# Splitting the side products of an attention kernel in two, and reordering its first unit's DMA queue

## The chip, the core and the metric

The kernel runs on one core of a Trainium2 chip. The time is that of the device, in microseconds (us), as the median of several runs. TensorE (PE) multiplies matrices into PSUM, ScalarE (ACT) takes the exponentials, VectorE (DVE) and GpSimd (POOL) do the elementwise work, and SyncE (SP) issues nearly all DMAs, in program order.

## What is computed

x has 4 batches of 1024 rows of 128 numbers. The reference, cut to what matters:

```python
q, k, v = ln(x) @ Wq, ln(x) @ Wk, ln(x) @ Wv
latent  = (k + v) @ W_down_kv
k, v    = latent @ W_up_k, latent @ W_up_v           # 16 heads of 8
s       = clip(q @ k.T * scale) * exp(-c * |i - j|)   # per head, 1024 x 1024
x       = x + (softmax(s) @ v) @ Wo
x       = x + bf16(fp8(ln(x)) @ fp8(kernel)) + bias   # fp8 rounding, scales are 1
```

64 score matrices of 1024 x 1024 need 67 million exponentials; they are the bulk of the work.

## The kernel before

**Units and quads.** The work is cut into 8 units: unit 2b + h holds the 512 queries of half h of batch b. A unit has 4 groups of 4 heads, and a group has 8 key chunks of 128. One group with one chunk is a **quad**, so a unit has 32 quads, numbered 0 to 31 within it, and the program has 256. A quad has two **slots**, each with the scores of two heads: 128 keys x 1024. One ACT instruction (L758) exponentiates a slot. Three pairs of PSUM banks hold the slots in turn, so the scores of slot s can be made when the exponential of slot s - 3 has ended.

**A quad on PE** (the loop from L964 on) is: scores of the even slot (`qk`, two matmuls that run together), the product of probabilities and values of two quads ago (`weigh`, four matmuls in two passes, L957), scores of the odd slot, and then, where the table `PE_SIDE` has the quad, a **side product** (`job`). Side products are the projections of the next batch (T = transposes of the normalised rows, k, q, v, and n = sums of squares of all heads) and the tail of the unit before (sp = spread of the softmax sums over a head's columns, proj = product with Wo, xqT and y for the fp8 product). All of them use one PSUM bank, `work`, so each waits until DVE has emptied it of the one before (`emptied`); DVE does this one quad later (`DVE_SIDE`). v and proj are four fp32 matmuls of 128 columns, k, q and sp one fp32 matmul of 512 columns, n four of 32 output rows each side by side in the array, T four transposes.

**The decay** is folded into queries and keys. It is exact off the diagonal block. In quads whose keys lie in the queries' own half (the even quads of a unit), DVE multiplies part of the scores by a correction before the exponential may start (`fix`, L1182): 2 x 256 columns in quads 2 and 4 of a group, here called **wide**, and 2 x 128 in quads 0 and 6, **narrow**. Odd quads need none.

**Group ends.** When the eight quads of a group are weighed, DVE copies the sums out of PSUM (`copy_pv`, L1190), and the first `weigh` of the next group, which stands in its quad 2, that is in quads 2, 10, 18 and 26 of a unit, waits for this copy. SP then sends the copy to tiles `den` and `o_raw` in 8 small DMAs (`gather`, L453 and L456). In quad 7 of the next unit DVE waits for the last of them, inverts the sums (L1195) and widens them (L1201); the corrections of quad 8 stand behind that on DVE.

**SP's queue** is written out by hand. In unit 0 it holds the gathers of each group, the stores of the keys and queries of batch 0 and 1 in three bf16 parts (L390, L398), and the loads that stage them for the groups (`stage`, L405, L413). **POOL** makes these parts (`split`), the normalised rows, and the end of the fp8 product. Before L698 it does, per batch: early keys and queries, the result of the unit before, late keys, late queries, squares for n.

## Time and profile before

| | |
|---|---|
| median of 3 runs | 534.98 us (530.42 to 535.65) |
| the profiled execution's own time | 534.09 us |
| its span, first to last instruction | 532.2 us |
| PE busy | 490.4 us (92%) |
| ACT busy | 490.8 us (92%), 512 exponentials |
| DVE, POOL busy | 280.6 and 218.8 us |
| mean granted TensorE clock | 0.985 |

PE and ACT are both busy 92% of the span. That is an average. A busy PE is read with care, since a matmul's record runs on while the next has begun; what counts for PE is the distance between the starts of successive blocks.

### The profile page before, as it was taken

To read this page: it belongs to the slowest core of one execution; us is meant where nothing else is said; L and a number is where in the kernel's file an instruction comes from. 1 tells how busy PE (TensorE), PEld (TensorE's weight loads), DVE (VectorE), ACT (ScalarE), POOL (GpSimd) and SP (SyncE) were. 2 spreads that over 40 slices of the span, in tenths; PEclk is the share of its full clock that TensorE was granted. 3 is DMA by queue.
4 is the path that set the end of the run, shared out by engine and by line. 5 is a ranking of instruction groups with operands and counts; after the bars stand their busy time and mean duration, and the time that the engine had idled before them with its cause. 6 is when DMAs were issued, how large, how long until landed. Compare 5 with 4: busy or idle time off the path is not lost.

```text
span 532.2 us, 9397 instructions
## 1 busy us (share of the span) xinstructions
PE 490.4 (92%) x3457; PEld 113.2 (21%) x3457; DVE 280.6 (53%) x641; ACT 490.8 (92%) x534; POOL 218.8 (41%) x285
## 2 busy tenths in 40 slices
PE   7799999899999999999999999999999999999961
PEld 3312111131122212221121211221111212122220
DVE  4524744455645564554744555554555645455646
ACT  3789999889999999999999999999999999999961
POOL 0889419791450229992251218993101211002110
PEclk9999999899999999999999999999999999999995
DMA  5589789837976102757967000757977000100000
GB/s 174 166 253 223 254 240 261 315 144 175 249 158 149 46 5 71 263 183 192 263 149 178 10 4 23 278 169 214 264 176 166 20 7 7 46 1 2 1 20 25
DMA packets 50467, 73.79 MB, mean 139 GB/s; under 512 B 6192, under 2 KB 29168, under 8 KB 50416
## 3 DMA queue, kind: packets, MB, share of 16 engines
q1 hardware_dynamic: 49600, 72.85, 49.5%
q8 instruction: 29, 0.48, 0.4%
q10 hardware_dynamic: 816, 0.28, 0.2%
q14 instruction: 22, 0.18, 0.1%
HBM read 35.40 MB, written 35.65 MB: 133 GB/s over the span
## 4 chain that ended last, share of the span: by engine, by line
PE 45%; ACT 34%; issue 9%; DVE 5%; DMA 3%; POOL 2%; SPq 1%; ACTq 0%; DVEq 0%; POOLq 0%
ACT probs L758 33%; PE ps L957 23%; PE ps L941 13%; DVE ps L1182 2%; PE ps L937 2%; PE ps L859 1%; PE ps L854 1%; PE ps L822 1%; PE ps L831 1%; DMA decay<-decay_rows 1%; PE ps L826 1%; DMA o_raw<-pv_out 1%; DMA wuv_s<-L_attn_W_up_v 1%; SPq L453 0%; POOL sq L584 0%
## 5 line engine op out<-in xcount | busy, mean ns | idle before, releaser
L758 ACT ACTIVATE probs<-ps 128x1024 f32<-128x1024 f32 x512 | 480.2, 1067 | 14.9 <-DVE ps L1182 9.4
L957 PE MATMUL ps<-probs,V 128*9 128x512 f32 x2048 | 268.6, 596 | 3.0 <-ACT probs L758 0.8
L1182 DVE TENSOR_TENSOR ps<-ps,consts 128x256 f32<-128x256 f32 (+1 forms) x256 | 143.9, 565 | 176.3 <-PE ps L941 169.3
L941 PE MATMUL ps<-Qs,Ks 64*128 64x512 bf16 x992 | 181.7, 386 | 16.6 <-ACT probs L758 8.4
L941 PEld LDWEIGHTS ps<-Qs,Ks 64*128 64x128 bf16 x992 | 43.9, 93 | 288.8 <-ACT probs L758 272.1
L645 POOL TENSOR_TENSOR xs<-xs,magic 128x512 f32<-128x512 f32 x7 | 8.9, 1277 | 96.2 <-DVE magic L1243 96.2
L957 PEld LDWEIGHTS ps<-probs,V 128*9 128x9 f32 x2048 | 31.3, 88 | 77.9 <-issue 57.6
L1190 DVE COPY pv_out<-ps 105x512 f32<-105x512 f32 x31 | 21.4, 691 | 33.7 <-PE ps L957 33.7
L562 POOL TENSOR_SCALAR rs<-mv 128x4 f32<-128x4 f32 (+1 forms) x10 | 2.3, 229 | 82.7 <-DVEq L1364 82.0
L596 POOL TENSOR_TENSOR sq<-sq,parts 128x1024 f32<-128x1024 f32 (+1 forms) x16 | 29.0, 1813 | 1.3
L598 POOL TENSOR_TENSOR parts<-sq,parts 128x1024 bf16<-128x1024 f32 (+1 forms) x16 | 28.3, 1771 | 1.3
L658 POOL TENSOR_TENSOR yb<-yb,bias_s 128x512 bf16<-128x512 bf16 x7 | 8.1, 1154 | 49.6 <-DVE yb L1315 49.2
L584 POOL TENSOR_TENSOR sq<-kT,decay 128x512 f32<-128x512 f32 (+2 forms) x13 | 16.2, 1246 | 28.5 <-DVE kT L1282 26.6
L589 POOL TENSOR_TENSOR sq<-qT,decay 128x1024 f32<-128x1024 f32 x7 | 16.6, 2366 | 3.5 <-DMA qp_dram<-parts 2.3
L595 POOL CAST parts<-sq 128x1024 bf16<-128x1024 f32 (+1 forms) x16 | 14.9, 933 | 1.0
L597 POOL CAST parts<-sq 128x1024 bf16<-128x1024 f32 (+1 forms) x16 | 14.4, 897 | 1.0
L937 PE MATMUL ps<-Qs 32*128 32x512 f32 x64 | 9.1, 637 | 3.2 <-ACT probs L758 2.6
L826 PE MATMUL ps<-xnT,wq_s 128*128 128x512 f32 x16 | 9.0, 643 | 0.8 <-ACT xnT L737 0.8
L822 PE MATMUL ps<-xnT,wk_eff 128*128 128x512 f32 x16 | 8.9, 638 | 0.8 <-ACT qT L743 0.8
L831 PE MATMUL ps<-wv_eff,xnT 128*128 128x128 f32 x64 | 9.3, 288 | 0.0
L646 POOL TENSOR_TENSOR xs<-xs,magic 128x512 f32<-128x512 f32 x7 | 8.9, 1278 | 0.5
L1098 DVE BATCH_NORM_STATS2 stats<-X 128x6 f32<-128x128 f32 x32 | 6.8, 278 | 3.3 <-DMA X<-L_attn_x 3.2
(148 smaller groups left out, 284.7 us busy)
## 6 DMA issues: line engine op xcount, KB each, us to landing
Qs<-qp_dram SPq DMA_DIRECT2D x26, 512.0 KB, 9.2
qp_dram<-parts SPq DMA_DIRECT2D x14, 768.0 KB, 4.6
Ks<-kp_dram SPq DMA_DIRECT2D x26, 384.0 KB, 5.5
kp_dram<-parts SPq DMA_DIRECT2D x12, 384.0 KB, 3.5
kp_dram<-parts SPq DMA_DIRECT2D x6, 768.0 KB, 5.2
qp_dram<-parts SPq DMA_DIRECT2D x7, 512.0 KB, 6.0
X<-L_attn_x SPq DMA_DIRECT2D x10, 256.0 KB, 3.3
Qs<-qp_dram SPq DMA_DIRECT2D x10, 256.0 KB, 9.5
```

The lines of the kernel that those rows point to most:

```text
L584: chain(nc.gpsimd.tensor_tensor(rest[:, at:at + n], kT[:, cols], decay[:, 1 - v, cols], ALU.mult))
L589: chain(nc.gpsimd.tensor_tensor(rest.rearrange("p (v n) -> p v n", v=2), q2, decay[:, :, cols], ALU.mult))
L595: chain(nc.gpsimd.tensor_copy(to[0], r))
L596: chain(nc.gpsimd.tensor_tensor(r, r, to[0], ALU.subtract))
L598: chain(nc.gpsimd.tensor_tensor(to[2], r, to[1], ALU.subtract))
L758: nc.scalar.activation(probs[:, quad % RING, 2 * jp:2 * jp + 2, :].rearrange("p j n -> p (j n)"), ps_all[:, bank * CH:(bank + 2) * CH], AC ...
L831: last = nc.tensor.matmul(bank[:, t * P:(t + 1) * P], xnT[:, at:at + P], wv_eff[:, :], start=True, stop=True)
L937: last = nc.tensor.matmul(bank, K0[group, g, kc * P:(kc + 1) * P], Q0[group, v, :], start=True, stop=True)
L941: last = nc.tensor.matmul(bank, Ks[half, g, jp, key_cols(v, kc)], Qs[half, g, jp, qh, v, :], start=True, stop=True)
L957: last = nc.tensor.matmul(pv[32 * j:32 * j + VW, :], V[:, unit // 2 * NB + kc, HG * j + g, :], probs[:, quad % RING, j, :], start=i == 0, ...
L1182: nc.vector.tensor_tensor(own, own, factors, ALU.mult).then_inc(fixed, 1)
L1190: nc.vector.tensor_copy(pv_out[0:96 + VW, group % 2, :], pv[0:96 + VW, :]).then_inc(pv_copied, 1)
```

## The change

Four things are changed.

1. **Split side products.** k, q, v, n, sp and proj (all but those of the first projections) are issued in two parts: the first and the second 256 columns, two of the four column blocks, or two of n's four matmuls. An entry of `JOBS` now has two places. A place that ends in .5 lies inside the quad that begins half a quad later, right behind the scores of its even slot and ahead of `weigh`. Only the last part signals, so DVE empties the bank once, as before.
2. **Other places.** Parts within a quad stand in quads 2, 10, 18 and 26. In a unit of the middle with odd number the places are: q at 2 (inside) and 2 (end), xqT at 4, y at 6, sp at 10 (inside, end), proj at 12 and 14, v at 18 (inside, end), the second v at 20 and 22, n at 26 (inside, end). With even number: xqT at 2 (inside), y at 4, T at 6, sp at 10 (inside, end), proj at 12 and 14, T at 18 (inside), k at 20 and 22, the second k at 26 (inside, end), q at 28 and 30. Row statistics of the tail move from 13 and 15 to 15 and 17, the last unit's transposes (`turn`) from 14, 18 and 26 to 18 (inside), 22 and 26 (inside), and the flags from 14 and 18 to 18 and 20.
3. **SP's queue in unit 0.** Late queries of batch 0 are stored before the gather of group 1 and not behind it; the early keys of batch 1 behind the gather of group 3 and not ahead of it; x of batch 2 is loaded behind the gather of group 2 and not ahead of that of group 1.
4. **POOL and DVE.** POOL makes the late keys before the result of the unit before, for batches 2 and 3. The preparation of the fp8 weights on DVE moves from quads 16 to 23 of unit 0 to 21 to 28.

```diff
-JOBS = [(FIRST_VALUES, "v", 0), (3, "v", 1), (10, "q", 1), (22, "n", 0)]
+JOBS = [(None, FIRST_VALUES, "v", 0), (None, 3, "v", 1), (None, 10, "q", 1), (20, 22, "n", 0)]
...
-        (10, "sp"), (12, "proj"), (TAIL_ROWS[_u], "xqT"), (TAIL_PRODUCTS[_u], "y"))]
+        (9.5, 10, "sp"), (12, 14, "proj"), (None, _rows, "xqT"), (None, _products, "y"))]
...
@@ SP, unit 0
                     store_qk(0)
+                    store_queries(0, "late queries", 1)
                 elif g == 1:
-                    store_queries(0, "late queries", 1)
...
-                    if qh == 0 and g == 2 and b < B - 1:
+                    if qh == 0 and g == (3 if b == 0 else 2) and b < B - 1:
                         store_keys(b + 1, "early keys", early, 0)
...
-                    if qh == 0 and g == 0 and b < B - 2:
+                    if qh == 0 and g == (2 if b == 0 else 0) and b < B - 2:
                         sp.wait_ge(tr_ps, 2 * b + 2)
                         load_x(b + 2)
@@ POOL
                     early_parts(b + 1)
+                    late_keys(b + 1)
                     if b > 0:
                         result(2 * b - 1)
-                    late_keys(b + 1)
@@ PE
+            def project_k(n, bank, part=None):
+                if part != 1:
+                    pe.wait_ge(xnT_ready, n + 1)
+                last = nc.tensor.matmul(columns(bank, part), wk_eff[:, :], xnT[:, own_rows(n, part)], start=True, stop=True)
+                if part != 0:
+                    last.then_inc(k_ps, 1)
...
+                for a in range(2) if part is None else (part,):
                     for half in range(2):
                         at = 64 * a + 32 * half
                         last = nc.tensor.matmul(bank[at:at + 32, :], hsum, sq[:, a, half * CH:(half + 1) * CH],
                                                 start=True, stop=True)
...
                     qk(s)
+                    if s % 2 == 0 and quad - 0.5 in PE_SIDE:
+                        job(*PE_SIDE[quad - 0.5])
                     if quad >= 2 and s % 2 == in_f32:
                         weigh(quad - 2)
...
@@ DVE
-                elif at == 13:
+                elif at == 15:
                     row_stats(unit)
-                elif at == 15:
+                elif at == 17:
...
-                if 16 <= quad < 24:
-                    prepare_weights(quad - 16)
+                if 21 <= quad < 29:
+                    prepare_weights(quad - 21)
```

What this does to the order of the instructions is shown at three places. The first is PE in unit 3, from quad 9 on. `ps<-Qs,Ks` are scores (x2 is one slot), `ps<-probs,V` is `weigh`, `ps<-wide,consts` is sp and `ps<-wo_s,OT` is proj. Before:

```order
L941 MATMUL ps<-Qs,Ks 128x512 x4
L957 MATMUL ps<-probs,V 9x512 x4
L941 MATMUL ps<-Qs,Ks 128x512 x2
L854 MATMUL ps<-wide,consts 128x512
L941 MATMUL ps<-Qs,Ks 128x512 x2
L957 MATMUL ps<-probs,V 9x512 x4
L941 MATMUL ps<-Qs,Ks 128x512 x4
L957 MATMUL ps<-probs,V 9x512 x4
L941 MATMUL ps<-Qs,Ks 128x512 x2
L859 MATMUL ps<-wo_s,OT 128x128 x4
L941 MATMUL ps<-Qs,Ks 128x512 x2
```

Changed:

```order
L972 MATMUL ps<-Qs,Ks 128x512 x4
L880 MATMUL ps<-wide,consts 128x256
L988 MATMUL ps<-probs,V 9x512 x4
L972 MATMUL ps<-Qs,Ks 128x512 x2
L880 MATMUL ps<-wide,consts 128x256
L972 MATMUL ps<-Qs,Ks 128x512 x2
L988 MATMUL ps<-probs,V 9x512 x4
L972 MATMUL ps<-Qs,Ks 128x512 x4
L988 MATMUL ps<-probs,V 9x512 x4
L972 MATMUL ps<-Qs,Ks 128x512 x2
L888 MATMUL ps<-wo_s,OT 128x128 x2
L972 MATMUL ps<-Qs,Ks 128x512 x2
```

Half of sp now stands ahead of quad 10's `weigh`, half behind its second scores, and half of proj where all of it stood. The second place is PE in unit 3 where n stands (`ps<-sq,consts`), before in quad 28:

```order
L957 MATMUL ps<-probs,V 9x512 x4
L941 MATMUL ps<-Qs,Ks 128x512 x2
L840 MATMUL ps<-sq,consts 32x512 x4
L941 MATMUL ps<-Qs,Ks 128x512 x2
L957 MATMUL ps<-probs,V 9x512 x4
```

Changed, in quad 26:

```order
L972 MATMUL ps<-Qs,Ks 128x512 x4
L863 MATMUL ps<-sq,consts 32x512 x2
L988 MATMUL ps<-probs,V 9x512 x4
L972 MATMUL ps<-Qs,Ks 128x512 x2
L863 MATMUL ps<-sq,consts 32x512 x2
L972 MATMUL ps<-Qs,Ks 128x512 x2
L988 MATMUL ps<-probs,V 9x512 x4
```

The four matmuls that stood together stand two and two, on both sides of a `weigh`. The third place is SP's queue in unit 0, behind the stores of k and q of batch 0. Before:

```order
L433 DMA kt_dram<-kT 128x1024
L435 DMA qt_dram<-qT 128x1024
L363 DMA X<-L_attn_x 128x8x128
L453 DMA den<-pv_out 8x1x64
L456 DMA o_raw<-pv_out 8x512
```

Changed:

```order
L436 DMA kt_dram<-kT 128x1024
L438 DMA qt_dram<-qT 128x1024
L401 DMA qp_dram<-parts 128x3x1024 x2
L401 DMA qp_dram<-parts 128x2x1024
L456 DMA den<-pv_out 8x1x64
L459 DMA o_raw<-pv_out 8x512
```

The store of the late queries has come ahead of the gather of group 1, and the load of x has gone from there.

## Rows read from the trace of the kernel before

**Rows 1.** Windows, units 1, 3, 4: length, busy PE, PEld, DVE, ACT, POOL, clock, DMA.

```profile
84.04:148.56 64.52, 60.35 (x426) 13.28 (x422) 34.00 (x78) 60.23 (x66) 39.48 (x50) 0.97 0.81 227
209.18:270.12 60.94, 58.94 (x426) 13.34 (x424) 33.97 (x79) 60.09 (x65) 38.93 (x51) 1.00 0.77 225
270.12:330.75 60.63, 59.20 (x422) 13.18 (x420) 32.48 (x65) 60.04 (x65) 20.27 (x28) 1.00 0.27 62
```

**Rows 2.** Timeline, ACT without gap: start, length, engine, line, operation, tiles, count.

```profile
373.23 14.85 ACT L758 ACTIVATE probs<-ps 128x1024 f32<-128x1024 f32 x16
```

**Rows 3.** Timeline of a wide quad (20 of unit 5), no side product near.

```profile
369.27 0.92 PE L941 MATMUL ps<-Qs,Ks 64*128 64x512 bf16 x4
369.70 0.70 DVE L1182 TENSOR_TENSOR ps<-ps,consts 128x512 f32<-128x512 f32 x1 [0.60 <-PE ps L941]
370.52 1.06 ACT L758 ACTIVATE probs<-ps 128x1024 f32<-128x1024 f32 x1
```

**Rows 4.** Groups by form: line, engine, shapes, count, busy us, mean ns, idle before.

```profile
L1182 DVE TENSOR_TENSOR ps<-ps,consts 128x256 f32<-128x256 f32 x128 | 54.8, 432 | 98.5 <-PE ps L941 95.9 <-PE ps L937 2.1 <-DVE mv L1224 0.5
```

**Rows 5.** Timeline of PE, unit 5: sp in quad 10, proj in quad 12.

```profile
349.94 1.12 PE L854 MATMUL ps<-wide,consts 128*128 128x512 f32 x2
350.47 0.59 PE L854 MATMUL ps<-wide,consts 128*128 128x512 f32 x1
351.00 0.39 PE L941 MATMUL ps<-Qs,Ks 64*128 64x512 bf16 x2
352.30 0.61 PE L941 MATMUL ps<-Qs,Ks 64*128 64x512 bf16 x4
353.81 0.39 PE L941 MATMUL ps<-Qs,Ks 64*128 64x512 bf16 x2
354.13 1.16 PE L859 MATMUL ps<-wo_s,OT 128*128 128x128 f32 x8
355.22 0.39 PE L941 MATMUL ps<-Qs,Ks 64*128 64x512 bf16 x2
```

**Rows 6.** Timeline of PE: n in unit 5; T in unit 4.

```profile
384.25 1.06 PE L840 MATMUL ps<-sq,consts 128*32 128x512 f32 x8
385.25 0.39 PE L941 MATMUL ps<-Qs,Ks 64*128 64x512 bf16 x2
304.15 0.65 PE L816 MATMUL ps<-eye,X 128*128 128x128 f32 x4
```

**Rows 7.** Timeline of quad 18 of unit 5: the copy at a group's end.

```profile
363.91 0.69 DVE L1190 COPY pv_out<-ps 105x512 f32<-105x512 f32 x1 [0.78 <-PE ps L957]
364.23 0.10 PEld L941 LDWEIGHTS ps<-Qs,Ks 64*128 64x128 bf16 x2 [0.37 <-ACT probs L758]
364.75 0.62 PE L957 MATMUL ps<-probs,V 128*9 128x512 f32 x4
```

**Rows 8.** Timeline of the stall in quad 8 of unit 1.

```profile
99.20 0.55 DVE L1195 RECIPROCAL rec<-den 128x64 f32<-128x64 f32 x1 [1.63 <-DMA o_raw<-pv_out]
99.61 1.16 POOL L596 TENSOR_TENSOR sq<-sq,parts 128x512 f32<-128x512 f32 x1
99.79 1.53 DVE L1201 TENSOR_TENSOR wide<-rec,consts 128x512 f32<-128x512 f32 x1
101.76 1.02 ACT L758 ACTIVATE probs<-ps 128x1024 f32<-128x1024 f32 x1 [2.23 <-DVE ps L1182]
```

**Rows 9.** Timeline of SP's queue; last row from the chain of waits.

```profile
63.85 2.07 SPq L398 DMA_DIRECT2D qp_dram<-parts  x3
70.92 1.32 SPq L405 DMA_DIRECT2D Ks<-kp_dram  x2
...
87.44 2.00 SPq L390 DMA_DIRECT2D kp_dram<-parts  x3
...
94.27 4.84 DMA o_raw<-pv_out
```

**Rows 10.** Timeline of unit 0: one DVE step of `prepare_weights`.

```profile
54.53 1.60 DVE L1150 TENSOR_SCALAR xs<-w_s,rscales 128x128 f32<-128x128 bf16 x1
```

More of the change, by code:

```diff
@@ L3 @@
 from contextlib import ExitStack
+import math
 F32 = mybir.dt.float32
@@ new lines @@
+    JOBS += [(_b * STREAM + 57.5, _b * STREAM + 58, "n", _b + 1)]
+JOBS += [(None, 3 * STREAM + 18, "flags", 0), (None, 3 * STREAM + 20, "flag", 0)]
+JOBS += [(None, (UNITS - 1) * UNIT_QUADS + _q, "turn", _g) for _g, _q in enumerate((17.5, 22, 25.5))]
+JOBS.sort(key=lambda _j: _j[1])
+LOOPED_UNITS = 2 * B
+JOB_ORDER = [(_k, _i) for _, _, _k, _i in JOBS] + [(_k, UNITS + _n) for _n in range(LOOPED_UNITS) for _k in ("proj", "xqT", "y")]
+PE_SIDE = {_q: (_k, _i, None if _f is None else 1) for _f, _q, _k, _i in JOBS}
@@ L146, in build @@
+PE_SIDE.update({_f: (_k, _i, 0) for _f, _, _k, _i in JOBS if _f is not None})
+assert len(PE_SIDE) == len(JOBS) + len([_j for _j in JOBS if _j[0] is not None])
+DVE_SIDE = {math.ceil(_q) + (_q > FIRST_VALUES): (_k, _i) for _, _q, _k, _i in JOBS}
+assert len(DVE_SIDE) == len(JOBS)
 def build(nc, x, wq, wkT, wvT, wo, wd, wuk, wuv, w8, s_in, s_k, bias, decay_rows, decay_table,
@@ L832, in project_v, with head_norms @@
                                             start=True, stop=True)
-                last.then_inc(v_ps, 1)
-            def head_norms(b, bank):
-                pe.wait_ge(sq_ready, b + 1)
-                for a in range(2):
+                if part != 0:
+                    last.then_inc(v_ps, 1)
+            def head_norms(b, bank, part=None):
+                if part != 1:
+                    pe.wait_ge(sq_ready, b + 1)
+                for a in range(2) if part is None else (part,):
                     for half in range(2):
@@ L841, in head_norms @@
                                                 start=True, stop=True)
-                last.then_inc(n_ps, 1)
+                if part != 0:
+                    last.then_inc(n_ps, 1)
             def turn_tops(bank):
@@ L850, in sum_oks, with spread_sums, project_o @@
                 nc.tensor.matmul(bank[0:1, 0:1], oks[:, 0:1], ones[:, :], start=True, stop=True).then_inc(flag_ps, 1)
-            def spread_sums(unit, bank):
-                pe.wait_ge(spread, unit + 1)
-                nc.tensor.matmul(bank, same_head, wide[:, :], start=True, stop=True).then_inc(spread_ps, 1)
-            def project_o(unit, bank):
-                pe.wait_ge(ot_ready, unit + 1)
-                for t in range(4):
+            def spread_sums(unit, bank, part=None):
+                if part != 1:
+                    pe.wait_ge(spread, unit + 1)
+                cols = slice(0, CH) if part is None else half_cols[part]
+                last = nc.tensor.matmul(bank[:, cols], same_head, wide[:, cols], start=True, stop=True)
+                if part != 0:
+                    last.then_inc(spread_ps, 1)
+            def project_o(unit, bank, part=None):
+                if part != 1:
+                    pe.wait_ge(ot_ready, unit + 1)
+                for t in range(4) if part is None else pairs[part]:
                     last = nc.tensor.matmul(bank[:, t * P:(t + 1) * P], OT[:, unit % 2, t * P:(t + 1) * P], wo_s[:, :],
                                             start=True, stop=True)
-                last.then_inc(proj_ps, 1)
+                if part != 0:
+                    last.then_inc(proj_ps, 1)
             def transpose_xq(unit):
@@ L902, in job @@
                 elif kind == "sp":
-                    spread_sums(i, work)
+                    spread_sums(i, work, part)
                 elif kind == "turn":
@@ L907, in job @@
                 elif kind == "proj":
-                    project_o(i, work)
+                    project_o(i, work, part)
                 elif kind == "xqT":
@@ L998, in _ @@
             weigh(QUADS - 1)
-            pairs = (range(0, 2), range(2, 4))
             for half in range(2):
```

56 lines of the change are left out of this document (25 added, 31 removed).

## The prediction

> **What bounds the kernel now.** I read the page first: ACT and PE are each busy 92% of the span, so neither can be called the bound from the averages. The windows by unit come next [rows 1]: units 3 and 4, in the steady part, last 60.94 and 60.63 us, unit 1 64.52. Against these stands ACT without a gap: 16 exponentials in 14.85 us, of which the last alone is about 1.06 us, so one each 0.92 us and 64 in 58.7 us [rows 2]. A middle unit loses 2.0 to 2.3 us to waits, unit 1 5.9 us. Only these losses can be won, and ACT's pace is the floor.
>
> Where they arise needs the timeline of a quad without side work [rows 3]. Two exponentials are 1.83 us, which is ACT's pace for a quad. On PE, in a quad where PE is late the step from scores to scores takes 352.30 to 353.81, 1.51 us [rows 5]. So PE catches up **0.31 us per quad**, and every side product makes it late. How late may it be? In the wide quad the correction of the odd slot ends at 369.70 + 0.70 = 370.40 and the exponential starts at 370.52; I take 0.03 of these 0.12 for the signal. The odd slot of a **wide** quad thus forgives **0.09 us**. A **narrow** correction lasts 0.43 and not 0.70 [rows 4], so it forgives 0.27 more; I use 0.31. An **uncorrected** quad forgives 0.70 more than the wide one, 0.80.
>
> **An account by hand.** Let D be PE's lateness at a quad's start. A side product at the end of a quad adds its own time plus 0.09 (scores to scores take 0.23, scores to side product 0.32 [rows 5]) and takes off 0.31 of recovery. What D exceeds the allowance of the next quads by is paid by ACT and leaves D. Before, sp takes 351.00 - 349.94 = 1.06, proj 355.22 - 354.13 = 1.09 [rows 5], n 1.00 [rows 6]. For sp in 10 and proj in 12: quad 10 pays 0.1 for the copy at the group's end and is 0.16 later by it; quad 11 D = 0.90, pays 0.10; wide quad 12 D = 0.49, pays 0.40; quad 13 pays 0.16; narrow 14 0.18. Sum 0.94. A second v in 14 pays 0.38 + 0.18, q and v in 4 and 6 of odd units 0.04 + 0.18 + 0.38 + 0.18, n in 28 only 0.16, because its next corrected quad is narrow. The whole account gives 2.6 for an odd unit and 2.35 for an even one; the trace has 2.3 and 2.0 [rows 1]. It is high by 0.3 in both, so I use differences alone.
>
> **The split parts.** A 512-column fp32 product is two passes, which start at 349.94 and 350.47, and the next scores follow at 351.00 [rows 5]. Each pass is 0.53. I estimate 0.43 of it for the 512 columns (two cycles each at the granted 2.4 GHz) and 0.10 as fixed, a weight load or the change to the next block. Half of its columns cost 0.10 + 0.43 + 0.10 = 0.63, so two parts are 1.26: splitting adds 0.2 us of PE time to each. Half a proj or v is 0.64. Bounds: 0.53 (exactly half) and 0.75 (every overhead doubled); I take 0.63 because the load stands in front of each of these products. n is different: its four matmuls run side by side in 1.00 us [rows 6], so two of them should take 1.00 as well, bounds 0.5 and 1.0; n doubles, to 2.0 us.
>
> **Parts inside quads 2, 10, 18, 26.** There PE waits for the copy: scores at 364.24, copy ends 363.91 + 0.69 = 364.60, `weigh` starts 364.75, which is 0.51 behind the scores and not 0.32 [rows 7]. The hole is only 0.19 us wide. A part of 0.63 in it delays `weigh` by 0.63 against a quad without either, and with it the odd scores of a *wide* quad, which forgives 0.09. ACT pays 0.54 at once, 0.91 for half an n, about 0.5 for T (its record is 0.65 [rows 6], some 0.06 of it beside the next block) and 0.24 for xqT (0.33). Afterwards PE is less late, which is what the spacing wins.
>
> - **sp and proj now**: quad 10 pays 0.54; the end part leaves D = 0.50 in quad 11, 0.19 in 12, which pays 0.10; proj's halves in 12 and 14 never pass the allowance (0.51 in 13, 0.63 in 15, 0.32 in 16, pays 0.01). Sum 0.65, was 0.94.
> - **Odd unit**: q in 2 with xqT, y behind it 0.64; sp, proj 0.65; v in 18, 20, 22 0.68; n 0.91 in quad 26, 0.08 in 27, 0.40 in wide 28, 1.39 in all, was 0.16. Sum 3.35, was 2.6: **+0.75** each for units 3 and 5.
> - **Even unit**: xqT 0.24, T in 6 nothing, sp, proj 0.65, T in 18 0.50, k in 20, 22 nothing, k in 26 0.54, q in 28, 30 0.10. Sum 2.03, was 2.35: **-0.3** each for units 2 and 4.
> - **Unit 6**: xqT 0.24 is new, 0.3 is won at sp and proj, and the flags' chain of small DVE steps now delays a wide quad (20) where it delayed a narrow one (16): **+0.2**. **Unit 7**: the transposes inside 18 and 26, of T's size, pay about 0.5 each, the latter after a copy it waits for; 0.3 won at sp: **+0.6**.
> - **Unit 0**: the weights' steps leave quads 16 to 23, where one of them took 1.60 us for 128 columns [rows 10] with corrections queued behind it; I put that at 0.8 us. At 21 to 28 POOL is idle. The k and q products of quads 26 to 30 cost 0.64 for 1.4; T inside 18 costs 0.5, n in halves 0.6 for 0.1. **-0.6**.
> - Row statistics two quads later leave POOL four quads (7.3 us) for 14 small steps of 0.3 us: nothing. POOL's late keys ahead of the result: late queries start at about the same time, since y is two to four quads later; nothing.
>
> **The stall in unit 1.** DVE stood 1.63 us until the last gather of unit 0 landed at 99.11 (94.27 + 4.84 [rows 9]); then came 0.55, and 1.53 for the widening, over twice its usual time. The exponential of quad 8 started 2.3 us late [rows 8]. PE idled, and in this unit the granted clock is 0.97 of full [rows 1], that is 3.4 us at 1.2 GHz, the lower of its two levels; it cost about 1.2 us in quads 10 and 11. Together 3.5 us, the estimate that unit 1's length against unit 3's confirms (64.52 - 60.94 = 3.6). In the new order the store of the late queries stands one gather (5.4 us of issue) and one load ahead of 63.85, so the staging loads, which wait for it, start some 3 us before 70.92. The last gather then does not wait for the 2.0 us issue of the early keys at 87.44 either, nor lie behind their 2 MB [rows 9]. I estimate its issue complete by 92 and its landing at 95 to 97, and DVE wants it at about 97.6. The wait goes.
>
> What is late next is the widening. It started at 99.79 while a POOL step ran until 99.61 + 1.16 = 100.77, and ended 0.55 behind that step [rows 8]: DVE stood until POOL was through. In the new order k's last projection of batch 1 comes two quads later, so POOL is then splitting the early queries in steps of up to 2.1 us. DVE has 0.3 us to spare; a mean wait of about 1 us plus 0.55 leaves a stall of about 1.3 us, too short for the clock to fall. Bounds 0 and 2.2. Unit 1 also gets the odd unit's +0.8. So 1.3 + 0.8 - 3.5: **-1.4**.
>
> By the Trainium skill, page "SBUF — State Buffer", section "Who interferes with whom", a DVE instruction with two SBUF inputs and a GpSimd one exclude each other for their whole length. The trace agrees (100.77 and then 0.55), and it is this rule that speaks for a rest of the stall.
>
> **Sum**: -0.6 - 1.4 - 0.3 + 0.75 - 0.3 + 0.75 + 0.2 + 0.6 = -0.3. Against the profiled execution's 534.1 us this is **533.8 us**. The median shown is 0.9 above that execution; I keep its own time.
>
> By the Trainium skill, "TensorE: Matmul & The Clock Gate", section "LDWEIGHTS" and its mechanism in Part 3, PE pulls weight loads ahead of running matmuls where row groups allow. Here the trace disagrees: the second pass starts 0.53 behind the first for 0.43 of columns [rows 5]. The rule would make the loads vanish behind the columns; what that gives is the rival of parts of exactly half.
>
> **Rivals.**
> - **As summed** (532 to 535.5), 0.40.
> - **The parts inside hide** (0.17). If the hole under load is longer than 0.19, since DVE's copy is later when PE is, a part of 0.63 pays 0.2 and not 0.54. There are 27 such parts in the 8 units; 27 x 0.25 = 6.8 us less: 527. Against it: rows 6 are quads where PE was on time, as it mostly is there.
> - **Parts of exactly half** (0.05): a part's fixed 0.10 is hidden, it costs 0.53 and not 0.63, 0.1 less at each of the 27 inside parts: 2.7 us less, 531. Against it stand both passes of 0.53.
> - **The stall goes wholly** (0.18): POOL's step ends in time. 1.3 us less, 532.5.
> - **Slower: the stall stays whole** (0.15). Its place is quad 8 of unit 1, its price the 2.1 us that I counted as won, and it decides once widening ends over 2.3 us late, by a late landing or a long POOL step. Then only the steady loss is left: 536. With the parts at 0.75 as well (0.12 more at some 27 places) 539.5.
> - **The change doesn't spread anything** (0.05): a second part waits for the bank's emptying. It doesn't by the code, which waits for first parts alone; time as before.
>
> **Chances.** What can be told from no change is about 1%, 5.3 us. Faster than 529.6 takes the hidden parts (0.17), or parts of half with the stall wholly gone and the bounds on its side (0.04): 0.21. Slower than 540.3 needs the whole stall and dear parts: 0.05. Within: 0.74. The range for 8 in 10 runs from 528.5, inside the hidden case, to 537.5.
>
> **What would show it.** After: exponentials of the odd slot in quads 2, 10, 18, 26 start 0.5 us late; blocks of n of 1.0 us each, twice; sp's halves 0.63 apart; units 3 and 5 longer by 0.7, unit 1 shorter by 1.4; no clock loss near 104; DVE's widening in unit 1 over 1 us. The prediction is wrong if `weigh` behind an inside part starts within 0.7 us of the scores, or if n's halves take 0.5.

## The result, and the profile after

The changed kernel takes 536.28 us (median, 533.6 to 539.36) and the kernel before 533.37 us (530.42 to 536.65) on the same chip: ratio 1.0044, 95% interval 1.0027 to 1.0061. By the medians that is 2.9 us slower, by the ratio 2.3 us (it is not the quotient of the two medians, which is 1.0055), where I forecast 0.3 us less. The time lies inside my range (528.5 to 537.5), but the sign is wrong, and a ratio of 1 lies outside the interval. The profiled execution of after is the longest of its 20: 539.36 us, span 537.5 us, 5.3 us above the 534.1 of the profiled execution before. I keep the two scales apart: terms are compared between traces, the whole between medians. So the stall that this trace shows below may be larger than what the median execution loses.

The page after, the instructions and the exponentials in section 5:

```profile
PE 496.2 (92%) x3495; PEld 119.6 (22%) x3495; DVE 275.9 (51%) x641; ACT 487.3 (91%) x534; POOL 219.1 (41%) x285
...
L763 ACT ACTIVATE probs<-ps 128x1024 f32<-128x1024 f32 x512 | 476.6, 1068 | 24.1 <-DVE ps L1212 20.6
```

ACT stands idle ahead of the exponentials for 24.1 us, where it was 14.9. 20.6 of it is put down to corrections (L1212), before it was 9.4. Which corrections these are, the windows by unit tell; they are to be compared with [rows 1]. Units 1 to 4, columns as there:

```profile
83.22:145.33 62.11, 60.48 (x434) 14.48 (x430) 34.14 (x79) 59.63 (x66) 43.83 (x54) 1.00 0.73 211
145.33:212.56 67.23, 61.93 (x424) 14.50 (x422) 31.89 (x64) 59.63 (x66) 19.43 (x27) 0.95 0.38 86
212.56:274.65 62.09, 60.30 (x438) 14.52 (x434) 34.06 (x80) 59.62 (x65) 39.90 (x52) 1.00 0.76 223
274.65:335.20 60.55, 59.18 (x424) 14.04 (x422) 32.01 (x64) 59.30 (x66) 19.43 (x27) 1.00 0.27 61
```

Unit 1 is 2.4 us shorter than before, unit 3 1.15 us longer, unit 4 as before, and **unit 2 lasts 67.23 us where it lasted 60.63**, with the granted clock at 0.95. All eight, each from its first exponential (L763, before L758) to the next unit's, unit 7 to the end of the last:

```
unit         0      1      2      3      4      5      6      7
before   68.46  64.51  60.63  60.94  60.63  60.94  60.00  59.76
after    68.06  62.11  67.23  62.09  60.55  61.69  59.46  60.37
differs  -0.40  -2.40  +6.60  +1.15  -0.08  +0.75  -0.54  +0.61
forecast -0.6   -1.4   -0.3   +0.75  -0.3   +0.75  +0.2   +0.6
```

Unit 2 alone misses its term by 6.9 us. The other seven sum to -0.9, against a forecast of 0.0 for these seven.

The stall of unit 1 [rows 8] is gone. Timeline of its quad 7 and 8 after:

```profile
96.42 0.54 DVE L1225 RECIPROCAL rec<-den 128x64 f32<-128x64 f32 x1
96.56 1.04 POOL L602 CAST parts<-sq 128x1024 bf16<-128x1024 f32 x1
96.99 1.15 DVE L1231 TENSOR_TENSOR wide<-rec,consts 128x512 f32<-128x512 f32 x1
97.67 2.46 POOL L603 TENSOR_TENSOR parts<-sq,parts 128x1024 bf16<-128x1024 f32 x1
98.06 0.42 DVE L1212 TENSOR_TENSOR ps<-ps,consts 128x256 f32<-128x256 f32 x1
```

The reciprocal has no wait in brackets any more. The widening takes 1.15 us, not 0.69: a POOL step runs beside it until 97.60, and it ends 0.54 us behind that step. The correction of quad 8 stands behind it, and ACT still runs through fifteen exponentials without a gap (from 89.30 to 103.26). In its place stands a new stall, a unit later. Timeline of quad 8 of unit 2:

```profile
162.78 0.55 DVE L1225 RECIPROCAL rec<-den 128x64 f32<-128x64 f32 x1 [4.82 <-DMA o_raw<-pv_out]
163.37 0.69 DVE L1231 TENSOR_TENSOR wide<-rec,consts 128x512 f32<-128x512 f32 x1
163.98 0.76 DVE L1212 TENSOR_TENSOR ps<-ps,consts 128x256 f32<-128x256 f32 x2
164.50 4.69 ACT L763 ACTIVATE probs<-ps 128x1024 f32<-128x1024 f32 x5 [4.11 <-DVE ps L1212]
...
166.50 0.61 PE L972 MATMUL ps<-Qs,Ks 64*128 64x512 bf16 x2 [0.31 <-ACT probs L763]
167.03 1.22 PE L880 MATMUL ps<-wide,consts 128*128 128x256 f32 x2
...
168.19 1.90 PE L988 MATMUL ps<-probs,V 128*9 128x512 f32 x8
```

DVE stands for 4.82 us until the last gather of unit 1 has landed, ACT for 4.11. Then the clock goes: half of sp takes 1.22 us and not 0.70, a `weigh` of eight 1.90 and not 1.05. One window over it, 164 to 174 us; the third number from the end is the granted clock, and behind it stands the busy share of the DMA engines:

```profile
164.00:174.00 10.00, 8.11 (x36) 1.90 (x40) 3.62 (x8) 7.08 (x8) 0.00 (x0) 0.66 0.31 84
```

The granted clock is 0.5 of full, the 1.2 GHz level, for 6.8 us from 165.2 (0.34 of the 10 us is missing, at half clock 6.8 us), after PE had idled through the stall. Quad 8 lasts 6.04 us and not 1.83, which is the wait, 4.2 us; quads 10 to 12 last 4.15, 2.18 and 2.25 where they last 2.34, 1.83 and 1.93 at full clock (unit 4 after), which is the clock's part, 2.5 us.

Why the gather landed so late stands in SP's queue and in the chain of waits. Timeline of SP, then the end of the chain in front of the stall:

```profile
145.17 1.31 SPq L408 DMA_DIRECT2D Ks<-kp_dram  x2
146.53 1.25 SPq L416 DMA_DIRECT2D Qs<-qp_dram  x2
147.82 0.70 SPq L456 DMA_DIRECT2D den<-pv_out  x1
```

```profile
152.66 10.03 DMA o_raw<-pv_out
```

A gather of 16 KB that took 4.84 us to land before, in the stall of unit 1 [rows 9], took 10.03. The staging loads of batch 1's second half (L408, L416; 1.8 MB) are issued right ahead of it. In the kernel before, the same gather was issued at 155.73, 3.1 us later, and had landed when DVE came for it at 159.98. So the gather is not issued late; what has grown is its time from issue to landing. The DMA engines are busy all of this time, from 145 to 163 us (share 1.03, next to last):

```profile
145.00:163.00 18.00, 16.20 (x124) 3.71 (x120) 6.67 (x12) 15.29 (x17) 5.32 (x5) 1.00 1.03 223
```

### The profile page after: what moved, and what is told of

Read it like the earlier page. It is cut to its first block, busy times and chain, and to the rows that moved or that the text cites. A ratio compares the mean times of both kernels' runs of the same rounds, so it can differ in the third digit from the quotient of the medians.

```text
span 537.5 us, 9480 instructions
## 1 busy us (share of the span) xinstructions
PE 496.2 (92%) x3495; PEld 119.6 (22%) x3495; DVE 275.9 (51%) x641; ACT 487.3 (91%) x534; POOL 219.1 (41%) x285
## 4 chain that ended last, share of the span: by engine, by line
PE 44%; ACT 32%; issue 9%; DVE 6%; DMA 4%; POOL 3%; SPq 2%; DVEq 0%; POOLq 0%; ACTq 0%
ACT probs L763 31%; PE ps L988 22%; PE ps L972 13%; DMA o_raw<-pv_out 2%; PE ps L880 2%; DVE ps L1212 2%; PE ps L844 1%; PE ps L851 1%; PE ps L863 1%; PE ps L839 1%; PE ps L888 1%; DMA Ks<-kp_dram 1%; DMA kp_dram<-parts 1%; DMA X<-L_attn_x 1%; PE ps L821 1%
## 5 line engine op out<-in xcount | busy, mean ns | idle before, releaser
L763 ACT ACTIVATE probs<-ps 128x1024 f32<-128x1024 f32 x512 | 476.6, 1068 | 24.1 <-DVE ps L1212 20.6
L1212 DVE TENSOR_TENSOR ps<-ps,consts 128x256 f32<-128x256 f32 (+1 forms) x256 | 144.1, 566 | 194.1 <-PE ps L972 186.6
L972 PE MATMUL ps<-Qs,Ks 64*128 64x512 bf16 x992 | 179.0, 386 | 18.1 <-ACT probs L763 11.3
L650 POOL TENSOR_TENSOR xs<-xs,magic 128x512 f32<-128x512 f32 x7 | 8.9, 1277 | 69.1 <-DVE magic L1273 69.1
L600 POOL CAST parts<-sq 128x1024 bf16<-128x1024 f32 (+1 forms) x16 | 14.9, 932 | 1.0
L844 PE MATMUL ps<-xnT,wq_s 128*128 128x256 f32 (+1 forms) x28 | 10.6, 460 | 0.8 <-ACT xnT L742 0.8
L839 PE MATMUL ps<-xnT,wk_eff 128*128 128x256 f32 (+1 forms) x28 | 10.5, 458 | 0.8 <-ACT qT L748 0.8
L851 PE MATMUL ps<-wv_eff,xnT 128*128 128x128 f32 x64 | 10.9, 297 | 0.0
L880 PE MATMUL ps<-wide,consts 128*128 128x256 f32 x28 | 10.8, 472 | 0.0
L888 PE MATMUL ps<-wo_s,OT 128*128 128x128 f32 x56 | 10.0, 300 | 0.0
```

Source lines behind the costliest of these rows:

```text
L763: nc.scalar.activation(probs[:, quad % RING, 2 * jp:2 * jp + 2, :].rearrange("p j n -> p (j n)"), ps_all[:, bank * CH:(bank + 2) * CH], AC ...
L844: last = nc.tensor.matmul(columns(bank, part), wq_s[:, :], xnT[:, own_rows(n, part)], start=True, stop=True)
L851: last = nc.tensor.matmul(bank[:, t * P:(t + 1) * P], xnT[:, at:at + P], wv_eff[:, :], start=True, stop=True)
L880: last = nc.tensor.matmul(bank[:, cols], same_head, wide[:, cols], start=True, stop=True)
L972: last = nc.tensor.matmul(bank, Ks[half, g, jp, key_cols(v, kc)], Qs[half, g, jp, qh, v, :], start=True, stop=True)
L1212: nc.vector.tensor_tensor(own, own, factors, ALU.mult).then_inc(fixed, 1)
```

## The experiments

**What the theories were.** Theory 1, for unit 2: the stall needs three things at once. The compute is 3.2 us earlier (unit 2 starts at 145.33, before at 148.56); POOL makes batch 1's k and q parts later, because in the new table k's second product of unit 0 is in quad 30 and q's first in 34, where they were in 28 and 30; and the staging loads lie ahead of the gather. The rivals: the new queue order does it alone, or the split work does. Theory 2, for the +1.15 in odd units: n is doubled by the split. Theory 3: parts inside quads 2, 10, 18, 26 are a loss by themselves, and the same work spaced apart elsewhere would be free.

Each ratio is to the kernel before on the same chip, but the experiments ran on three chips: the first four on one, queue_late_stage, n_whole, t_end and spread_q on a second, sp_spaced and q_spaced on a third. The kernel before took 533.68, 534.08 and 534.24 us there. A difference of medians across two of these groups therefore carries some 0.5 us that is not the kernel's, and where I give one, the lengths of the units in the two traces say more.

### Split jobs with the old queue

The changed kernel, with SP's order as it was:

```diff
-                    store_queries(0, "late queries", 1)      # ahead of the gather of group 1
+                    store_queries(0, "late queries", 1)      # behind it
...
-                    if qh == 0 and g == (3 if b == 0 else 2) and b < B - 1:
+                    if qh == 0 and g == 2 and b < B - 1:
...
-                    if qh == 0 and g == (2 if b == 0 else 0) and b < B - 2:
+                    if qh == 0 and g == 0 and b < B - 2:
```

> The changed kernel with SP's queue of unit 0 as it was before. Theory 1 (the changed kernel loses 4.8 us in quad 8 of unit 2 because the last gather of unit 1 lands behind staging loads, after POOL's parts and with them the whole queue came 3.6 us later and compute 3.3 us earlier): unit 1 stalls again as before (64.5 to 66 us long), so that compute comes later and the stall in unit 2 shrinks to 0 to 2 us; median 535 to 538. Rival (the new order of SP's queue by itself makes the stall in unit 2): unit 2 is 60.5 us, with no wait for a gather, and the median is 534 to 535.5.

539.59 us (539.57 to 539.62), ratio 1.0118 [1.009, 1.0147]: the slowest of all, above the 535 to 538 expected. Unit 2 is back at 60.54 without a wait: it starts at 151.50, 6.2 us later than in the changed kernel. Unit 1 has the stall, larger than before the change (68.59 us). Timelines of DVE and of SP's queue, then the gather in the chain of waits:

```profile
100.97 0.55 DVE L1224 RECIPROCAL rec<-den 128x64 f32<-128x64 f32 x1 [4.78 <-DMA o_raw<-pv_out]
```

```profile
90.34 2.02 SPq L393 DMA_DIRECT2D kp_dram<-parts  x3
```

```profile
98.91 1.97 DMA o_raw<-pv_out
```

The stall's return to unit 1 was foretold, its size not. The store of the early keys, ahead of the last gather, starts at 90.34 where it was at 87.44 [rows 9]: 2.9 us later. The last gather behind it is issued 4.6 us later, lands 1.8 us later (100.9, before 99.1) and is wanted 1.4 us earlier (96.2, before 97.6), which gives 4.78 us of wait where it was 1.63. So the later products of k feed straight into unit 1, and the new queue order is what keeps them out of it.

### The queue alone

The kernel before with only the three changes on SP (the diff above, the other way).

> The kernel before with only SP's queue of unit 0 in the new order. Theory 1: the stall in unit 1 goes (unit 1 61.0 us, not 64.5), POOL is not late, so the last gather of unit 1 lands near 158 where compute wants it at 156.6; a stall in unit 2 of 0 to 1.5 us; median 1.5 to 3.5 us under the kernel before. Rival (the queue's order makes the stall): unit 2 loses 4 us or more in quad 8, median as before or over it.

531.28 us (530.21 to 533.78), 0.9964 [0.9945, 0.9983]. Unit 1 goes from 64.51 to 61.08. Unit 2 goes from 60.63 to 61.39: a small stall has come up there, and the granted clock stays full. ACT stands 0.78 us in it, DVE 2.34:

```profile
158.46 0.55 DVE L1195 RECIPROCAL rec<-den 128x64 f32<-128x64 f32 x1 [2.34 <-DMA o_raw<-pv_out]
```

Unit 2 starts at 144.60, 4.0 us earlier than before, and POOL is not later (the late queries are stored at 114.68, before at 114.39). So earlier compute alone brings the landing of unit 1's last gather into the path (wanted at 156.1, before at 159.98; it takes 6.59 us to land), and the queue order is worth about 2 us as it is. Unit 1's gain of 3.4 us is what its stall was worth; I had put it at 3.5.

### The gather ahead of the staging loads

The changed kernel; staging of group 2 of batch 1 waits until the last gather is issued:

```diff
-                    if qh == 1 and b < B - 1:
+                    if qh == 1 and b < B - 1 and not (b == 0 and g == 2):
                         sp.wait_ge(qk_done, 2 * NB * (group + 1))
+                        if b == 0 and g == 3:
+                            stage(b + 1, 2)
                         stage(b + 1, g)
```

> The changed kernel, with the staging loads of group 2 of batch 1 issued behind the last gather of unit 1 and not ahead of it. Theory 1: the gather has one group's loads (2 x 384 and 2 x 512 KB) less before it, lands near 154, ahead of need (158), and unit 2 falls from 67.2 to 60.5 us with the clock at its full level throughout; median 5 us under the changed kernel's slow executions and 3 to 4 us under its median. Rival (POOL or the copy is what is late, not the loads ahead): unit 2 keeps over 3 us of its stall.

532.54 us (531.96 to 533.02), 0.9988 [0.9972, 1.0004]. Unit 2 is 60.54, its clock full, and no other unit has moved by more than 0.2 us except unit 0, -0.3:

```profile
144.94:205.49 60.55, 59.19 (x424) 14.06 (x422) 32.00 (x64) 59.30 (x66) 19.47 (x27) 1.00 0.39 90
```

The loads ahead of the gather were needed for the stall: it is issued at 152.04, 0.6 us earlier than in the changed kernel, and no wait for it is left. The median falls by 3.7 us, and the times of single runs, spread over 5.8 us in the changed kernel, now lie within 1.1. That fits a landing that decides by a small margin in each run whether there is a stall; it is an argument, since only one execution of each is traced.

### k and q of unit 0 whole and earlier

The changed kernel, with the k and q products of batch 1 unsplit, and all but the first two to four quads earlier:

```diff
-        ... (20 if _b else 25.5, 22 if _b else 26, "k", 0),
-        (25.5 if _b else 28, 26 if _b else 30, "k", 1), (28 if _b else 33.5, 30 if _b else 34, "q", 0),
-        (33.5 if _b else 36, 34 if _b else 38, "q", 1), ...
+        ... (20 if _b else None, 22 if _b else 26, "k", 0),
+        (25.5 if _b else None, 26 if _b else 28, "k", 1), (28 if _b else None, 30, "q", 0),
+        (33.5 if _b else None, 34 if _b else 36, "q", 1), ...
```

> The changed kernel with batch 1's k and q products whole and where they were before (quads 26, 28, 30, 36), so that POOL can make the parts of batch 1 some 3 us earlier. Theory 1: SP's gather of group 0 of unit 1 starts near 116.5 and not 120, the last gather of unit 1 lands 3 to 4 us earlier, and the stall in unit 2 falls from 4.8 to 1.5 us or less; unit 0 with its three products close together loses 0.8 us more; median 1 to 3 us under the changed kernel. Rival (the order of the queue alone): the stall keeps over 3.5 us.

532.92 us (532.41 to 536.55), 0.9996 [0.9977, 1.0016]; unit 2 60.55, no wait. The median is 3.4 us under the changed kernel's, where I expected 1 to 3. One range end, 536.55, is not explained by the traced execution. The first POOL step on k's second product stands in these timelines, of before, of the changed kernel and of this one:

```profile
78.08 2.63 POOL L584 TENSOR_TENSOR sq<-kT,decay 128x256 f32<-128x256 f32 x2 [18.11 <-DVE kT L1282]
```

```profile
81.30 2.63 POOL L589 TENSOR_TENSOR sq<-kT,decay 128x256 f32<-128x256 f32 x2 [21.75 <-DVE kT L1312]
```

```profile
77.50 2.63 POOL L589 TENSOR_TENSOR sq<-kT,decay 128x256 f32<-128x256 f32 x2 [17.97 <-DVE kT L1312]
```

Two quads of PE (3.66 us) make POOL 3.2 us later, and that runs on through SP: the store of batch 1's late queries, in unit 1, is at 114.39 before, 118.04 in the changed kernel, 113.75 here, and what is behind it follows: three gathers and the staging loads. The loads next ahead of the last gather start at 145.17 in the changed kernel and at 141.24 here. The last gather itself is issued at nearly the same time in both, 152.66 and 152.43: here SP waits for DVE's copy before it, in the changed kernel it comes to it straight from the loads. What the earlier loads give it is DMA engines that have room. DVE of this version, and its window 150 to 158:

```profile
157.73 0.54 DVE L1225 RECIPROCAL rec<-den 128x64 f32<-128x64 f32 x1
```

```profile
150.00:158.00 8.00, 7.64 (x64) 1.90 (x56) 4.14 (x9) 7.94 (x9) 2.32 (x2) 1.00 0.73 166
```

DVE comes at 157.73 and does not wait, so the gather took at most 5.3 us where it took 10.03; by the trace's completion records it landed at 157.41, 0.3 us before it was wanted. This cure holds by a small margin, which would fit the one execution of 536.55, though that one was not traced.

Either cure suffices, so the stall of 4.8 us needs both POOL's lateness and the loads ahead of the gather. That it needs the earlier compute too is seen in split_old_queue, where unit 2 starts late and has no stall. Neither rival holds: the new queue order by itself gives a small stall, the split work with the old order none in unit 2. Theory 1 holds, with one correction: compute that is earlier still (4.0 us, queue_only) brings 2.34 us of DVE's wait, 0.78 of ACT's, without POOL's lateness.

### The queue alone, with the gather ahead

queue_only with the staging edit.

> The kernel before with SP's queue of unit 0 in the new order, and the staging loads of group 2 of batch 1 behind the last gather of unit 1; side products as before. Theory (both stalls are the last gather's landing, nothing else): no wait for a gather in units 1 and 2, unit 1 61.0 us, unit 2 60.6 us instead of 61.4, median 0.7 to 1 us under that with the new queue alone, so 3 to 3.5 us under the kernel before. Rival (loads behind the gather are then late for quad 16 of unit 2): a new wait on a DMA in unit 2, no gain.

530.63 us (530.13 to 530.98), 0.9941 [0.9919, 0.9964]. Unit 2 is 60.63 as before, unit 1 61.09. This is what the queue's part of the change is worth once its own follow-up stall is taken out: 3.45 us of median. It also weighs the split jobs with their new places: with the same queue, late_stage takes 532.54, 1.9 us more between two chips (1.6 by the sum of the eight units).

### n in one piece

From here every kernel has the staging edit. n goes back to quad 28 (unit 0: 22), unsplit:

```diff
-JOBS = [... (20, 22, "n", 0)]
+JOBS = [... (None, 22, "n", 0)]
...
-    JOBS += [(_b * STREAM + 57.5, _b * STREAM + 58, "n", _b + 1)]
+    JOBS += [(None, _b * STREAM + 60, "n", _b + 1)]
```

> The changed kernel with the staging loads behind the gather, and n whole again, at the end of quad 28 (22 in unit 0). Theory 2 (half an n takes as long as a whole one, and its first half delays a wide quad at once): units 1, 3 and 5 fall from 62.1 to 60.8 us, unit 0 by 0.4 us, median 3.5 to 4.5 us under the kernel with n in halves, near 528.5. Rival (halves cost half, the loss of odd units comes from the parts of q, sp and v inside quads): under 1 us.

528.84 us (527.76 to 529.07), 0.9900 [0.987, 0.9931]. Against late_stage units 1, 3 and 5 shorten by 1.3, 1.3 and 1.05, 3.6 us in all; the medians, on two chips, differ by 3.7. Unit 0 shortens by 0.1 where I expected 0.4. Unit 3:

```profile
204.29:265.10 60.81, 59.47 (x438) 14.37 (x434) 34.09 (x80) 59.51 (x66) 39.58 (x51) 1.00 0.76 223
```

PE's busy time in it is 0.8 us less than in the changed kernel (60.30). n in the changed kernel, unit 5, timeline of PE:

```profile
382.59 0.90 PE L972 MATMUL ps<-Qs,Ks 64*128 64x512 bf16 x4
383.42 0.62 PE L863 MATMUL ps<-sq,consts 128*32 128x512 f32 x2
383.58 0.60 PE L988 MATMUL ps<-probs,V 128*9 128x512 f32 x2
383.87 0.60 PE L863 MATMUL ps<-sq,consts 128*32 128x512 f32 x2
384.01 1.32 PE L988 MATMUL ps<-probs,V 128*9 128x512 f32 x6
385.26 0.39 PE L972 MATMUL ps<-Qs,Ks 64*128 64x512 bf16 x2
385.58 1.05 PE L863 MATMUL ps<-sq,consts 128*32 128x512 f32 x4
386.57 0.39 PE L972 MATMUL ps<-Qs,Ks 64*128 64x512 bf16 x2
```

The half at the end stands from 385.58 to 386.57: 0.99 us for two matmuls, as long as the 1.00 of all four [rows 6]. Theory 2 holds.

### T, xqT and the transposes at the ends of quads

On top of it:

```diff
-    _rows, _products = (28, 30) if not is_shared(_u) else (33.5, 36) if _u % 2 else (36, 38)
+    _rows, _products = (28, 30) if not is_shared(_u) else (34, 36) if _u % 2 else (36, 38)
...
-        ... (None, 17.5, "T", 1), ...
+        ... (None, 18, "T", 1), ...
...
-... for _g, _q in enumerate((17.5, 22, 25.5))]
+... for _g, _q in enumerate((18, 22, 26))]
```

> As the one with n whole, and everything that was whole but stood inside quads 2, 18 and 26 (xqT, T, the last unit's transposes) now at the end of the same quads. No splitting is changed. Theory 3 (an inside part delays the odd scores of a wide quad, which forgives 0.09 us, by its full length; the hole at the group's end covers 0.19): units 2 and 4 fall by 0.5 to 0.6 us, unit 6 by 0.2, unit 7 by 0.6, unit 0 by 0.3; median 2 to 2.5 us lower. Rival (the hole hides inside parts, so at the end they cost more): same or slower.

525.31 us (525.05 to 526.23), 0.9845 [0.9815, 0.9875]. Units 2 and 4 lose 0.6 us each (4: 60.48 to 59.88), unit 7 0.8, unit 0 1.1, unit 6 0.2: 3.5 us of median, more than expected. The window of unit 4 and, from the page, the exponentials:

```profile
263.35:323.23 59.88, 59.12 (x424) 13.96 (x422) 32.00 (x64) 59.09 (x65) 19.95 (x28) 1.00 0.30 68
```

```profile
L765 ACT ACTIVATE probs<-ps 128x1024 f32<-128x1024 f32 x512 | 474.8, 1071 | 11.7 <-DVE ps L1214 9.0
```

ACT's idle time ahead of them is 11.7 us, against 24.1 in the changed kernel and 14.9 before. Quad 18 with T at its end lasts 1.85 us, with T inside 2.29: the same operation costs 0.02 at the free end beside the place where it cost 0.46, and 0.06 in quad 20.

### q at two ends, and y out of the way

```diff
-    _rows, _products = (28, 30) if not is_shared(_u) else (34, 36) if _u % 2 else (36, 38)
+    _rows, _products = (28, 30) if not is_shared(_u) else (34, 36) if _u % 2 else (34, 40)
...
-        (33.5 if _b else 36, 34 if _b else 38, "q", 1), ...
+        (36, 38, "q", 1), ...
```

> As the one before, and in odd units the second q in halves at the ends of quads 4 and 6, xqT at the end of 2 and y at the end of 8, so nothing stands inside quad 2. The account by hand gives odd units 3 and 5 0.1 us for 0.64 there: 0.5 us less each, 1 us less in all, near 525.5. Rival (POOL's result, late by y's two quads, makes late queries late): no gain, waits on POOL's parts in SP's queue.

526.65 us (525.95 to 527.05), 0.9866 [0.9836, 0.9896]: 1.3 us more than t_end, where 525.5 was expected (units 3 and 5 are 0.4 us longer each). Quads 0 to 7 of units 3 and 5 are free of any loss (1.83 us each), as the theory said. But quad 10 went from 2.34 to 3.34. Its timeline:

```profile
219.40 0.69 DVE L1222 COPY pv_out<-ps 105x512 f32<-105x512 f32 x1 [1.22 <-PE ps L990]
220.00 0.74 DVE L1347 TENSOR_SCALAR yb<-ps,oscale 128x512 bf16<-128x512 f32 x1
220.66 0.69 DVE L1214 TENSOR_TENSOR ps<-ps,consts 128x512 f32<-128x512 f32 x1
220.80 0.70 PE L882 MATMUL ps<-wide,consts 128*128 128x256 f32 x2 [0.93 <-DVE yb L1347]
221.43 1.04 PE L990 MATMUL ps<-probs,V 128*9 128x512 f32 x8
```

With y in quad 8, DVE empties the bank in quad 9, behind the copy of the group's end, and sp inside quad 10 waits 0.93 us for it. The cause is not the one I had named as a rival; a part inside a quad has a second price that end parts don't have, the emptying half a quad earlier.

### sp at two ends

t_end with half of sp in quad 8, the other at the end of 10: `(9.5, 10, "sp")` becomes `(8, 10, "sp")`.

> As the one with T, xqT and the last unit's transposes at quad ends, with sp's halves at the ends of quads 8 and 10, no longer inside 10. The account by hand gives 0.2 us for sp and proj where it gave 0.65 (0.61 in the traces): 0.35 to 0.4 us less in each of units 1 to 7, 2.5 to 3 us in all, near 522.5. Rival (sp in quad 8 then waits for the widened sums, which DVE makes in quad 7 behind the last gather): a wait in quad 8, no gain.

525.34 us (525.01 to 525.82), 0.9834 [0.9811, 0.9858]: the same as t_end, where I expected 522.5. Quad 10 still lasts 2.34. Its timeline in unit 4:

```profile
278.54 0.70 PE L882 MATMUL ps<-wide,consts 128*128 128x256 f32 x2
...
280.47 0.61 PE L974 MATMUL ps<-Qs,Ks 64*128 64x512 bf16 x4
280.61 0.69 DVE L1222 COPY pv_out<-ps 105x512 f32<-105x512 f32 x1 [1.52 <-PE ps L990]
281.22 0.69 DVE L1214 TENSOR_TENSOR ps<-ps,consts 128x512 f32<-128x512 f32 x1
281.45 1.04 PE L990 MATMUL ps<-probs,V 128*9 128x512 f32 x8 [0.37 <-ACT probs L765]
```

The half in quad 8 cost nothing there, but it makes PE half a us late (the scores of quad 10 at 280.47, in t_end at 279.50, where the exponentials themselves stand 0.46 us apart), and so also the last `weigh` of the group, the copy behind it (280.61) and the `weigh` behind that, which starts 0.98 us after the scores and not 0.51 [rows 7]. Whether half of sp lies in this hole or the hole is half a sp longer is the same. My account has the hole fixed at 0.19; it grows with PE's lateness. Theory 3 holds for T and for q, not for sp.

### q and sp at two ends

sp_spaced with q in 2 and 4 (both ends) and xqT and y of the shared units in 0 and 6.

> As the one before, and around units 3 and 5 xqT at the end of quad 0, q's halves at the ends of 2 and 4, y at the end of 6, so that sp does not wait for DVE emptying y as it did with y in quad 8. The account gives 0.3 us for 0.61 in units 3 and 5: 0.6 us less in all. Rival (xqT in quad 0 meets the lateness of q's half in quad 30 and costs as much): no change.

525.29 us (525.11 to 525.88), 0.9834 [0.9811, 0.9857]. Quad 2 of unit 3 is 2.22 and not 2.34, unit 3 0.12 shorter. The reason looks the same: xqT in quad 0 makes PE late, the copy of quad 2 follows, and `weigh` starts 0.93 us behind the scores (206.55 after 205.62) with nothing in between. The gain, 0.24 us of 0.6 expected, is far below what a median can tell.

The lengths of the quads of unit 3 that lose anything (1.83 is none), from the ends of the odd exponentials:

```
quad          2     4     6     7     8    10    11    12    13-14    15    16    18    20    24    26    28
before        .     .  1.97  2.25  1.98  1.90  1.94  2.25  1.98 x2  2.24  1.98  1.90     .     .     .     .
changed    2.34  1.94     .     .     .  2.34     .  1.93     .        .     .  2.35  1.94  2.02  2.58  2.48
n_whole    2.34  1.94     .     .     .  2.34     .  1.93     .        .     .  2.35  1.94  2.02     .     .
spread_q      .     .     .     .     .  3.34     .  1.93     .        .     .  2.35  1.95  2.02     .     .
q_spaced   2.22  1.93     .     .     .  2.34     .  1.93     .        .     .  2.35  1.94  2.02     .     .
```

Left out: 1.91 in quad 30 of all but the changed kernel (n in 28), 1.87 in quad 27 of the changed one.

The best versions, t_end, sp_spaced and q_spaced, are level at 525.3 us: 1.6% under the kernel before and 11 us, 2%, under the change.

## Why the prediction was wrong

**The account of the quads held.** sp and proj cost 0.51 in quad 10, where half of sp stands inside, and 0.10 in quad 12, where I had 0.54 and 0.11; T inside 0.46 to 0.47 (0.5), xqT 0.21 (0.24). Halves of sp and proj take 0.63 and 0.64 on PE, as worked out. Timeline of unit 3 after, which answers to [rows 5]:

```profile
229.90 0.39 PE L972 MATMUL ps<-Qs,Ks 64*128 64x512 bf16 x2
230.22 0.70 PE L880 MATMUL ps<-wide,consts 128*128 128x256 f32 x2
230.85 1.04 PE L988 MATMUL ps<-probs,V 128*9 128x512 f32 x8
```

`weigh` starts 0.95 behind the scores; the sign I had given for being wrong was under 0.7. The rivals of hidden parts and of exactly half are out: a part inside pays in full, and a half takes 0.63 us, not 0.53. What the first of them rested on, a hole that grows when PE is late, is real all the same (0.66 in sp_spaced); it had no place here, because PE is on time at these quads.

On one reading the prediction goes wrong. It held that the trace disagrees with the rule on pulled-ahead weight loads in the Trainium skill ("TensorE: Matmul & The Clock Gate", section "The mechanism"). The load of sp's second pass is in fact pulled ahead. Timeline of PEld before:

```profile
350.05 0.19 PEld L854 LDWEIGHTS ps<-wide,consts 128*128 128x128 f32 x1
```

It runs from 350.05 to 350.24, inside the first pass, which starts at 349.94; the second pass still starts only at 350.47 [rows 5]. So the pull-ahead is seen and does not shorten this product. Of the 0.53 us of a pass about 0.43 go with its columns, since halving the columns of both passes takes 1.06 us down to 0.63. What the other 0.10 is, no run here shows.

**n** costs 0.75, 0.04 and 0.65 us in quads 26 to 28 of unit 3, 1.44 where I had 1.39. The doubled block was right, and it is the largest loss of the steady part. What was mis-sized is the difference: the account gives 3.35 us for an odd unit and 2.03 for an even one, and they lose 3.4 and 1.85 (62.09 and 60.55 less 58.7). For before it was 0.3 high in both, and I had taken this error as common to both kernels. It was not: in the new layout the account is right to 0.2. That it belonged to the chains of late quads of the old layout is my reading; it was not tested. So unit 3 is +1.15 for +0.75 and unit 4 -0.1 for -0.3.

**Units 0, 6, 7** came out at -0.4, -0.5 and +0.6 for -0.6, +0.2 and +0.6. The 0.2 of unit 6 came from the flags, which I had costing more in wide quad 20 than in narrow quad 16. Before, quad 16 lasted 2.47, so they cost 0.64 there; now quad 20 lasts 1.85, so they cost almost nothing. Which of the two moves, the place or the earlier steps, freed them was not tested.

**The stall in unit 1** went, as the forecast said, and more than it said. I had 1.3 us left for the widening's wait for POOL's port, and it was not paid: the widening did run beside POOL, 1.15 us instead of 0.69, but DVE came to the reciprocal 1.2 us before my 97.6 (the last gather, issued at 90.36, had landed), and no exponential had to wait. That rival (532.5, 0.18) was right in its place. The widening alone takes 0.69 us and has taken 1.53 [rows 8] and 1.15 beside POOL, and both times it ended 0.54 to 0.55 us behind the POOL step that ran when it started. So the rule of the Trainium skill's page "SBUF — State Buffer" ("Who interferes with whom") is borne out, and it decides only where there is no slack.

**The failed step is the one on what is late next:** "The wait goes. What is late next is the widening." I followed the unit whose stall was removed, and not the transfer that comes next on the same path. Two omissions feed it. One is that unit 2 would start 2.0 us earlier by my own terms for units 0 and 1 (3.2 us in the trace) while the gather's landing need not move with it. The other is in the change's list: POOL "nothing", late queries "at about the same time", and k two quads later was counted only as PE's time. Through POOL it makes the store of late queries, the first three gathers of unit 1 and the staging loads behind them 3.4 to 3.7 us later. Nothing in unit 1 or 2 has to wait for that until the last gather. It is issued 3.1 us earlier than before, but into DMA engines that are still busy with the loads, and so takes 10.03 us instead of 2.0. It had a margin of about 2.3 us before (landed at 157.7, wanted at 159.98) and had to meet a demand 2.0 us earlier with a landing 5.0 us later. The clock's fall then turns a wait of 4.2 us into 6.7. The runs show it: taking away the loads in front of the gather or POOL's lateness removes the whole stall, and the median with the staging edit alone, 532.54 us, is 0.12% below the kernel before (interval -0.28% to +0.04%), where I forecast 0.06%.

My rival for a slower kernel had the stall staying whole at quad 8 of unit 1 (536, 0.15). The number 536 was met by luck: the place was one unit early, and the cause another one, not a stall that stays but one that is handed on.

**What stays open.** How much of the changed kernel's spread (533.6 to 539.4) is this race, since only one execution of each kernel was traced; the one of the changed kernel is its longest. And why unit 0 gains 0.4 and not 0.6, a difference below what I can tell from two traces.

## What to carry to other kernels

When a change removes a wait, write down for the next few transfers of the same kind when each is wanted and when it lands, and move the wanted times by what was won: a stall that is taken out of one round can come back in the next whose margin is smaller than what was won. Moving a product on the matrix engine can cost nothing there and yet delay every store, gather and load that is queued behind its result, so follow it through the queue to the first consumer that waits. And split a side product only where its halves are cheaper than the whole: halves of a stream of columns cost 0.63 us for 0.53, halves of a group packed side by side cost twice as much together, and a place inside a quad is dearer than a free end.

## What the runs showed that I had not expected

- The weight load of sp's second fp32 pass runs inside the first pass (350.05 to 350.24, first pass from 349.94), and yet the passes start 0.53 us apart.
- Two of the four matmuls of n that stand side by side take 0.99 us, as long as all four [rows 6]. In front of a `weigh` they let it in between their passes: its first two matmuls start at 383.58, between n's blocks at 383.42 and 383.87. How much time that saves the half inside was not measured; its quad still loses 0.75 us.
- A small gather behind bulk loads landed 10.03 us after its issue, with the DMA engines fully busy, in the same queue in which it took 4.84 [rows 9] and, for the last gather of unit 0 in split_old_queue, 1.97 us.
- The copy at the group's end follows PE's lateness, so the hole in front of `weigh` grew from 0.19 to 0.66 us (0.98 less 0.32) when half of sp was put two quads ahead of it.
